# Two chunks of a depthwise convolution multiplied one stage earlier

## What is computed

```python
def conv2d(x, w, b, groups=1):
    out = jax.lax.conv_general_dilated(x, w, window_strides=(1, 1), padding='SAME', ..., feature_group_count=groups)
    return out + b[None, :, None, None]
...
xz = jnp.einsum('bhwc,oc->bhwo', x, in_proj_w)       # 96 -> 384 channels
xi, z = jnp.split(xz, 2, axis=-1)                    # 192 and 192
xi = jax.nn.silu(conv2d(xi, conv_w, conv_b, groups=D_INNER))   # depthwise 3x3
...
x_dbl = jnp.einsum('bkdl,kcd->bkcl', xs, x_proj_w)   # projections of xi for the scan
out_y = selective_scan(xs, dts, A, Bs, Cs, ...)      # four directions over L = 4096
```

## Time and profile before

| what | value |
|---|---|
| time, median of 3 runs | 13456.75 us (13454.54 to 13469.53) |
| the profiled execution's own time | 13459.71 us |
| its span on the core | 13457.9 us |
| mean granted TensorE clock | 0.901 of full |
| busy: PE, DVE, ACT, POOL | 79%, 89%, 51%, 77% |
| one image (the second), span | about 1676 us |

### The profile page before, as it was taken

The page is one execution under the profiler, slowest core; times in us unless marked ns, Lnnn a source line. Parts: engine busy times, 40 slices in busy tenths (PEclk is TensorE's granted clock), DMA queues, the critical chain, the costliest instruction groups (busy, mean ns, idle before and its releaser), DMA issues. The chain is left out here.

```text
span 13457.9 us, 95099 instructions
## 1 busy us (share of the span) xinstructions
PE 10568.0 (79%) x24646; PEld 4131.8 (31%) x24646; DVE 11944.1 (89%) x8647; ACT 6832.9 (51%) x10172; POOL 10383.8 (77%) x4597
## 2 busy tenths in 40 slices
PE   6877877778777787777878778777787777877778
PEld 2333323333233332333323333233332333323333
DVE  7999779997799968999679996799968999679996
ACT  4545454554545545555455555555555545555455
POOL 4999459994599945999459994599946999369993
PEclk8899989999899998999989999899998999989999
DMA  4676446774467644677446774477735777357773
GB/s 140 216 219 215 114 131 215 218 214 112 136 214 220 214 107 140 214 219 216 102 143 216 220 214 99 145 216 220 214 96 152 214 220 213 95 151 214 220 214 94
DMA packets 734799, 2404.31 MB, mean 179 GB/s; under 512 B 173200, under 2 KB 175248, under 8 KB 722768
## 3 DMA queue, kind: packets, MB, share of 16 engines
q1 hardware_dynamic: 734192, 2397.58, 61.2%
HBM read 2300.18 MB, written 67.11 MB: 176 GB/s over the span
## 5 line engine op out<-in xcount | busy, mean ns | idle before, releaser
L1262 POOL TENSOR_TENSOR state<-state,c_sb 128x1024 f32<-128x1024 f32 x3072 | 7184.0, 2359 | 463.4 <-ACT carry L1089 461.7
L1018 PE MATMUL ps<-state,wt 128*128 128x512 f32 x12288 | 6328.2, 657 | 165.2 <-ACT ya L1082 107.8
L1018 PEld LDWEIGHTS ps<-state,wt 128*128 128x128 f32 x12288 | 2553.2, 211 | 3051.2 <-issue 2474.3
L1221 DVE TENSOR_TENSOR_SCAN state<-decay,carry,ps 128x1024 f32<-128x1024 f32 x1440 | 3379.2, 2347 | 104.2 <-DVE ps L1208 36.6
L1089 ACT COPY carry<-state 128x1 f32<-128x1 f32 x3072 | 585.3, 191 | 4860.5 <-DVE state L1221 4851.6
L995 PE MATMUL ps<-parts,sel 114*128 114x512 bf16 (+1 forms) x3840 | 1286.3, 420 | 2103.2 <-DVE state L1221 2101.9
L1251 POOL TENSOR_TENSOR dbu<-b_sb,du 128x1024 f32<-128x1024 f32 x1152 | 2719.1, 2360 | 231.0 <-DVE du L1236 231.0
L1208 DVE TENSOR_TENSOR ps<-ps,du 128x1024 f32<-128x1024 f32 x1920 | 2322.2, 1209 | 1.7 <-PE ps L995 0.8
L1131 ACT ACTIVATE decay<-delta,a_neg 128x1024 f32<-128x1024 f32 x1920 | 2194.8, 1144 | 6.9
L1221 DVE TENSOR_TENSOR_SCAN state<-ps,carry,dbu 128x1024 f32<-128x1024 f32 x864 | 2013.1, 2330 | 3.8 <-POOL dbu L1251 2.5
L995 PEld LDWEIGHTS ps<-parts,sel 114*128 114x128 bf16 (+1 forms) x3840 | 260.9, 100 | 3653.2 <-DVE state L1221 3385.8
(11 more groups left out here) (217 smaller groups left out, 10216.9 us busy)
## 6 DMA issues: line engine op xcount, KB each, us to landing
c_sb<-bc SPq DMA_DIRECT2D x2048, 512.0 KB, 4.4
c_sb<-bc SPq DMA_DIRECT2D x2048, 256.0 KB, 5.5
b_sb<-bc SPq DMA_DIRECT2D x768, 512.0 KB, 4.7
b_sb<-bc SPq DMA_DIRECT2D x768, 256.0 KB, 5.4
x_nat<-x SPq DMA_DIRECT2D x17, 1536.0 KB, 14.3
gates<-gate_a SPq DMA_DIRECT2D x8, 2048.0 KB, 6.8
x_tok<-x SPq DMA_DIRECT2D x288, 48.0 KB, 1.8
gn<-gn_t SPq DMA_DIRECT2D x8, 1536.0 KB, 7.1
```

The lines of the kernel that those rows point to most:

```text
L1018: mm = pe.matmul(py[:, q * CH:(q + 1) * CH], col("ident"), state[:, slot(g, n), q * CH:(q + 1) * CH], start=(n == 0), stop=False)
L1221: dve.tensor_tensor_scan(state[:, slot(g, n), way], rate, what, 0.0 if fresh else carry[:, n:n + 1], ALU.mult, ALU.add)\
L1262: pool.tensor_tensor(state[:, slot(g, n), :], state[:, slot(g, n), :], c_sb[:, n % CRING, :], ALU.mult).then_inc(S["weighted"], 1)
```

## The change

The five matmuls of chunk 0 and the five of chunk 1 leave `prep_b` and go into `prep_a`, into the same bank (`ps0`, which `turn` has used before). GpSimd's five instructions that make `conv_diag` now raise a semaphore, on which the first of the moved matmuls waits. The waits of the other engines are as they were: VectorE's `a_taps(0)` still waits for `conv_mm` of at least 1.

```diff
@@ prep_a, gpsimd
                         pool.tensor_tensor(conv_diag[:, t, :], col("ident"), conv_w[:, t:t + 1].broadcast_to([128, 128]),
-                                           ALU.mult)
+                                           ALU.mult).then_inc(S["pads_zero"], 1)
@@ prep_a, tensor
+                    def first_conv(s):
+
+                        if s == 0:
+                            pe.wait_ge(S["pads_zero"], 2 + PE_TAPS)
+                            pe.wait_ge(S["gn_scaled"], NCH)
+                            pe.wait_ge(S["xi_out"], 3)
+                        for t in range(PE_TAPS):
+                            mm = pe.matmul(ps2[0][:, s * CH:(s + 1) * CH], conv_diag[:, t, :],
+                                           pad_a[:, rows(s, t // 3), t % 3:t % 3 + W],
+                                           start=(t == 0), stop=(t == PE_TAPS - 1))
+                        if s == SLOTS - 1:
+                            mm.then_inc(S["conv_mm"], 1)
+
                     staggered((0, turn),
+                              (3, lambda j: first_conv(0) if j == NCH - 1 else None),
+                              (5, lambda j: first_conv(1) if j == NCH - 2 else None),
@@ prep_b, tensor
-                    for i in range(NCH // SLOTS):
+                    for i in range(1, NCH // SLOTS):
```

## The result

| | before | changed |
|---|---|---|
| median us (8 runs each) | 13456.62 | 13498.63 |
| lowest to highest | 13450.94 to 13469.53 | 13494.31 to 13504.54 |
| own time of the profiled execution | 13459.71 | 13494.31 |
| span in it, mean granted clock | 13457.9, 0.901 | 13492.4, 0.898 |

The ratio is 1.0033 (95% interval 1.0023 to 1.0043): the changed kernel is slower by 0.33%, 42 us. Between the two profiled executions it is 34.6 us, against 35.4 worked out. Every time in this document is of executions at the usual clock, except that one of the twelve of the change with the new order took 22286.53 us at a mean granted clock of 0.522, which moves the median of those twelve by 0.2 us.

A forecast was written before the change was run, and what follows sets the result against it. The prediction took the last `in_proj` ending `prep_a` and VectorE's path through `a_taps(0)` and GpSimd's sums in `prep_b` as bounds: 42.7 - 7.3 = +35.4 us, 13495.1 for the profiled execution, 13492 as median; range 13479 to 13512.

The forecast's parts named there:

- `prep_a` is longer, +42.7 us: End of `prep_a`: moved matmuls delay the last `in_proj`, +52.6 us over eight images, less 9.9 us from restored full clock.
- the 2.03 us of free time: Between `in_proj(6)` and `in_proj(7)` on TensorE: 2.03 us of the moved 8.60 us cost nothing, 6.57 us an image do.
- The 4.25 taken from before: End of `prep_a`: 4.25 us expected from the last `in_proj`'s L612 to the start of `prep_b` in all eight images.
- The wait ahead of `a_taps(0)` vanishes and brings little, -7.3 us: In `prep_b`: VectorE's wait goes, but GpSimd's sums hold it until 30.8 us; four images save 1.82 us each.
- the forecast's price: VectorE on `conv_acc` in `prep_b`: arriving at 22.2 instead of 23.2 us gains nothing; the step ends at 30.8 us.
- the sterner reading: Rival, `conv_acc` in `prep_b`: VectorE and GpSimd exclude each other for whole instructions, 0.6 us later an image; +37 to +42, chance 0.22.
- The late projections cost nothing: TensorE in `prep_b` after `u_out(2)`: half-clock projections' delay goes into the wait for `ur`; cost 0, up to 4 us.
- The 107.5 us of the prediction: In `prep_b`: TensorE's claimed total wait over the run for the last piece of the transfers.
- the forecast's +30 to +37: Whole kernel: the band around the summed +35.4 us, given chance 0.40.

The follow-up runs named there:

- the change with the new order: Against the change: in `prep_b`, `a_taps(2)` goes ahead of the nine `r_tap` on `conv_acc`, `u_out(2)` and the last gate ahead of the `ur` pieces; 13440.07 us.
- The version with four matmuls: Against the change: only taps 0 to 3 of chunk 0 moved ahead of the last `in_proj`, the other six left in `prep_b`; 13458.65 us, 1.0001 to before.
- the kernel before with the new order: Against the kernel before: no matmul moved, `a_taps(2)` ahead of the nine `r_tap`, `u_out(2)` and last gate ahead of the `ur` pieces; 13436.85 us.
- the one with nine: Against the change: two matmuls ahead of `in_proj(6)`, four ahead of `in_proj(7)`, three behind it, one left in `prep_b`; 13469.45 us, 1.001 to before.

## Why the prediction was right, step by step

**`prep_a` is longer, +42.7 us: right.** Measured +41.8 in the profile. Its two parts hold too: the added work counts less the 2.03 us of free time (8.59 us moved), and the last `in_proj` runs at full clock in all eight images, 4.14 to 4.15 us to `prep_b`. The 4.25 taken from before was 0.1 us too much, which over eight images is most of the 0.9 us between the two sums. The version with four matmuls shows both again with another amount.

**The wait ahead of `a_taps(0)` vanishes and brings little, -7.3 us: the mechanism right, and in this profile 4.3 us reach the end of the stage.** The step behind `conv_acc` starts at 30.7 in all images, as written. The start of the `ur` product, counted from the start of `prep_b`, moved by 7.8 us in sum over eight images, from 58.7 to 60.7 before to 58.6 to 59.3. But from `prep_b`'s start to the scan's first matmul the sum fell by only 4.3 us (670.4 to 666.1): behind the wait for `ur` 3.6 us were lost again. The granted clock shows where. These are the first 5.2 us from the start of that product in the fifth image, before and changed (clock in the last column but two):

```profile
6869.96:6875.16 5.20, 5.20 (x7) 2.12 (x8) 1.28 (x2) 2.07 (x5) 5.20 (x2) 0.64 1.04 183
6895.43:6900.63 5.20, 5.20 (x6) 2.16 (x7) 1.28 (x2) 1.58 (x3) 5.19 (x2) 0.50 0.88 159
```

From the start of that product to the scan's first matmul the clock was at half for 34.6 us in sum over eight images before and for 47.0 in the change, and the stretch took 192.4 and 196.0 us. In the version with all ten behind the last `in_proj`, whose `prep_b` has the same instruction lists as the change, it was at half for 33.9 us, the stretch took 192.9, and `prep_b` was 9.3 us shorter than before. In the one with the matmuls done twice, whose `prep_b` has the lists of before, it was at half for 44.1 us and the stretch took 195.8. So the 3.6 us go with the clock and not with the list. The forecast counted nothing for the clock behind the wait; why it stays at half longer in one image than in another I have not isolated.

**How VectorE and GpSimd shut each other out: the forecast's price held, and the sterner reading's was too high.** L859 was held for 1.02 us, all of its early arrival, but it ended when it had ended before, not 0.2 us later; the 0.6 us more per image did not come. The Trainium skill's page "SBUF — State Buffer", section "SBUF: two separate sides", says that VectorE in a two-port mode or with two SBUF inputs and GpSimd hold their shared ports by an exclusive lock for the whole instruction, while the other blocks fully. L859 reads one tile of SBUF, and no row shows its mode; its being held fits, with 1.51 us for an instruction of 0.49. But VectorE ended 23.63 us into the stage, with GpSimd's seventh sum running from 22.1 to 23.3 by its record (1.27 us a sum), so the hold was over some 0.2 us ahead of that record's end. That lead is where the reading by whole instructions went 0.2 us astray at this step. Times of GpSimd in the profile are rough, so it isn't shown whether the hold ended early or the record ends late; the price is what the row shows.

**The late projections cost nothing: right in its size.** 0.46 us of ScalarE's wait in four images, and TensorE's matmuls still wait 40.4 us over the run for `ur`. The 107.5 us of the prediction were read wrongly: they count each wait on the weight load and on the matmul, and the matmuls waited 47.0. No term of the sum hung on it.

**The predicted time** was 13492 for a measured 13498.6. Between the two profiled executions the sum is within 1 us, and that is in part luck: the two stages came out at +41.8 - 4.3 = +37.5, and the rest of the images, which the change doesn't touch, took 2.9 us less. One execution of the kernel before shows 1581 to 1587 us from image to image there, from the scan's first matmul to the last L623 of the next image's `in_proj(6)`. The profiled execution of before was 3 us above its median and that of the changed kernel 4.3 below, which makes 42 us out of 34.6; for these 7 us no trace is kept, and they lie well inside the interval of the ratio, 31 to 58 us. By its number the 42 us stand at the upper end of what was given to the sterner reading (+37 to +42) and not in the forecast's +30 to +37. The times can't tell these two apart. What speaks for the forecast is L859, which ended at 23.63 us, and the next step at 30.7.

## What to carry to other kernels

Here work moved ahead of a stage's border was free only in the gap where the engine waited, and only as much as the gap held: 2.0 us, and 8.6 were put in. Before moving work to end a wait, look at what the waiting engine does next: VectorE gave up a wait for TensorE and took up the same microsecond as a wait for GpSimd. An order of steps that avoids GpSimd and releases the long transfers early was worth 20 us alone, 51 us on the version with four matmuls moved and 59 us on the change: here the early matmuls paid only where VectorE asked for them early, and four of them, which fit the gap but for 1.4 us, did so at no cost in `prep_a`.

## What was unexpected in the hardware

A gap of 1.87 us in TensorE's work was followed by half clock in six of eight images before, in five of eight in the kernel before with the new order, and in all eight with the ten matmuls behind it. In the versions in which matmuls filled it (the change, the one with four, the one with nine and those built on them) no image had a drop there. In the kernel before the drop cost 1.6 to 1.7 us each time in `prep_a`, and in four of the six images 2.7 us more of TensorE's time at the start of `prep_b`, so that moving 3.4 us of work into a gap of 2.0 came out at no cost.
